# Attention and mixture layer on one core: the projection stage gets x already turned, and normalises it in that layout

## What is computed

```python
def _layernorm(x, axis=-1, eps=1e-05):
    m = jnp.mean(x, axis=axis, keepdims=True)
    v = jnp.var(x, axis=axis, keepdims=True)
    return (x - m) / jnp.sqrt(v + eps)
# x is 2 x 2048 x 512, Wq, Wk, Wv, Wo are 512 x 512, 16 heads of 32
q = split_heads(x @ Wq.T)
k = split_heads(x @ Wk.T)
v = split_heads(x @ Wv.T)
q = _rope(q)
k = _rope(k)
scores = jnp.einsum('bhqd,bhkd->bhqk', q, k) / math.sqrt(dk)   # causal, softmax, @ v, @ Wo.T
x = x + _L0_attn_ref(_layernorm(x, axis=-1), Wq, Wk, Wv, Wo)
x = x + _L0_ffn_ref(_layernorm(x, axis=-1), ...)               # a base product, a router, 8 LoRA experts
```

## Time and profile before

| | us |
|---|---|
| median of 3 runs | 1550.93 |
| lowest and highest | 1549.51, 1551.12 |
| profiled execution | 1550.66 |
| its span | 1548.9 |
| TensorE busy in the span | 1523.7 (98%) |
| VectorE busy | 1132.8 (73%) |
| GpSimd busy | 890.5 (57%) |
| ScalarE busy | 756.4 (49%) |

### The profile page before, as it was taken

One profiled execution on the slowest core, in us unless ns is written; L12 is line 12 of the kernel. 1 busy time (PEld: TensorE's weight loads), 2 busy tenths in 40 slices (PEclk: granted clock), 3 DMA queues, 4 the chain that ended last, 5 costly groups with the idle time before them and its releaser, 6 DMA issues.

```text
span 1548.9 us, 24844 instructions
## 1 busy us (share of the span) xinstructions
PE 1523.7 (98%) x9088; PEld 989.2 (64%) x9088; DVE 1132.8 (73%) x2269; ACT 756.4 (49%) x1540; POOL 890.5 (57%) x597
## 2 busy tenths in 40 slices
PE   7999999999999999999999999999999999999999
PEld 5888887755555555555555555555555547777777
DVE  6765656878877777777777878777777677666655
ACT  3222222135656656666666656665665673232221
POOL 2233332446878788888888797887797721121111
PEclk9999999979999999999999999999999999999999
DMA  5655685782476377468368359358445363223311
GB/s 204 211 190 204 207 266 185 225 187 61 90 167 148 83 160 162 89 140 182 84 137 191 83 127 202 83 116 197 100 99 134 88 147 109 82 82 105 134 61 55
DMA packets 120403, 215.83 MB, mean 139 GB/s; under 512 B 12504, under 2 KB 45784, under 8 KB 113112
## 3 DMA queue, kind: packets, MB, share of 16 engines
q1 hardware_dynamic: 102384, 136.20, 32.6%
q0 software_dynamic: 8064, 58.72, 18.4%
q10 hardware_dynamic: 9840, 19.40, 3.5%
HBM read 96.23 MB, written 58.72 MB: 100 GB/s over the span
## 4 chain that ended last, share of the span: by engine, by line
PE 92%; DVE 4%; DMA 2%; issue 1%; SPq 1%; ACT 1%; POOL 0%; POOLq 0%; DVEq 0%; ACTq 0%
PE a_mx L260 16%; PE a_st L1014 16%; PE a_av L1027 16%; PE p_pair L518 11%; PE f_wo_ps L1370 6%; PE p_v L530 5%; PE f_out_ps L1430 5%; PE a_sum L260 3%; PE a_sum L1049 2%; PE a_sum L1057 2%; DVE a_part L275 2%; PE f_out_ps L1445 1%; PE f_mid_ps L1370 1%; PE f_lg_ps L1400 1%; DMA a_gather<-a_pair 1%; PE a_mx L264 1%
## 5 line engine op out<-in xcount | busy, mean ns | idle before, releaser
L1114 ACT ACTIVATE a_probs<-a_st 128x512 f32<-128x512 f32 (+2 forms) x1244 | 573.6, 547 | 355.9 <-PE a_st L1014 347.2
L275 DVE TENSOR_REDUCE a_part<-a_mx 128x1 f32<-128x512 f32 (+2 forms) x773 | 495.4, 680 | 91.7 <-PE a_mx L260 78.9
L963 POOL TENSOR_TENSOR a_pair<-a_probs 128x1024 f32<-128x1024 f32 (+2 forms) x224 | 401.8, 1835 | 31.7 <-issue 16.4
L963 POOL TENSOR_TENSOR a_gather<-a_probs 128x1024 f32<-128x1024 f32 x76 | 179.9, 2388 | 84.5 <-ACT a_probs L1114 84.5
L392 POOL TENSOR_TENSOR p_rot<-p_mul 128x1024 f32<-128x1024 f32 x32 | 87.5, 2736 | 193.7 <-DVE p_mul L696 193.7
L1363 POOL TENSOR_TENSOR f_x<-f_x,f_bias 128x512 f32<-128x512 f32 x32 | 40.1, 1287 | 204.9 <-DVE f_xn L1580 204.9
L1027 PE MATMUL a_av<-a_probs,a_v 128*32 128x512 f32 (+3 forms) x1280 | 141.0, 540 | 2.2 <-POOL a_probs L944 2.2
L1027 PE MATMUL a_av<-a_probs,shared 128*32 128x512 f32 (+3 forms) x1280 | 142.6, 545 | 0.0
L278 DVE CUSTOM_DVE_ANT_0 a_mx<-a_mx,f_ctx 128x512 f32<-128x512 f32 (+1 forms) x155 | 94.7, 630 | 51.5 <-PE a_mx L260 51.5
L944 POOL TENSOR_SCALAR_AFFINE_SELECT a_probs<-a_probs 128x512 f32<-128x512 f32 x128 | 88.4, 755 | 64.2 <-ACT a_probs L1114 62.3
L1014 PE MATMUL a_st<-a_q_stack,a_k_stack 98*128 98x512 f32 (+3 forms) x287 | 101.8, 372 | 1.1 <-DMA a_q_stack<-a_neg_rows 1.1
(11 more groups left out here) (238 smaller groups left out, 3062.7 us busy)
## 6 DMA issues: line engine op xcount, KB each, us to landing
a_gather<-a_pair POOLq DMA_DIRECT2D x56, 1024.0 KB, 7.2
qk_scratch<-p_rot_hi SPq DMA_DIRECT2D x32, 512.0 KB, 3.1
qk_scratch<-p_rot_lo SPq DMA_DIRECT2D x32, 512.0 KB, 3.9
a_k_stack<-qk_scratch SPq DMA_DIRECT2D x60, 256.0 KB, 8.1
a_q_first<-qk_scratch SPq DMA_DIRECT2D x48, 256.0 KB, 7.0
a_third<-qk_scratch SPq DMA_DIRECT2D x36, 256.0 KB, 5.4
v_scratch<-p_v_st SPq DMA_DIRECT2D x32, 256.0 KB, 7.4
ctx_scratch<-a_ctx_st SPq DMA_DIRECT2D x32, 256.0 KB, 3.5
```

The source lines that it names most:

```text
L275: dve.tensor_reduce(found, scores.rearrange("p (h n) -> p h n", n=width), AX.X, ALU.max).then_inc(self.max_done, 1)
L963: pool.tensor_tensor(place[:, h:h + 2, q0:TT], probs[:, s % RING, h:h + 2, q0:TT], probs[:, (s + 1) % RING, h:h + 2, q0:TT], ALU.add).then ...
L1114: act.activation(probs[:, s % RING, h, q0:TT], score_bank(g, HG * s + h)[:, q0:TT], ACT.Exp, scale=SCORE_SCALE).then_inc(exp_done, 1)
```

## The change

The kernel gets x a second time, turned (features as rows, `x_t`, made like the turned weights before the launch). From tile 1 on: statistics come from `xb`, now one buffer, as before; the reciprocal goes into the variance's place in `mv`, so that mean and reciprocal lie side by side; SP stores `mv` (4 KB) to `row_scratch` in memory, waits for it, and loads it back spread to all 128 partitions as `rows_b` (4 KB in each, `spread_rows`). The turned tile `xt_raw` (1 MB, in the second x buffer's place) is loaded by ScalarE's queue at the end of a tile. GpSimd subtracts the mean from all 2048 elements of a partition in one instruction (`centre`, after rope sum 0), VectorE multiplies by the reciprocal in one (`scale`, after `rot_rest` 0). ScalarE's four `xt_copy` stand together after `rot_copy` 1, VectorE's four `xt_rest` together before `rope_mul` 3, both reading SBUF instead of PSUM. The transposes of tiles 1 to 7 are gone; tile 0 is turned as before.

```diff
-        xb = first.x
+        xb, xt_raw, rows_b = first.x[:, 0], first.x[:, 1], first.cin[:, 2:4, :].rearrange("p a n -> p (a n)")
-        rstd = sb("p_rstd", [P, SUB])
+        rstd = mv[:, :, 1]
+        mean_row, rstd_row = (rows_b.rearrange("q (p s c) -> q s p c", s=SUB, c=2)[:, :, :, c].unsqueeze(1).to_broadcast([P, KT, SUB, P])
+                              for c in range(2))
+        xt_tokens = xt_raw.rearrange("q k (s p) -> q k s p", p=P)
...
+            def centre(T):
+                pool.wait_ge(rows_loaded, 16 * T)
+                pool.wait_ge(xt_loaded, 16 * T)
+                pool.tensor_tensor(xt_tokens, xt_tokens, mean_row, ALU.subtract).then_inc(centred, 1)
             with pool.Fori(0, TILES - 1) as T:
                 for p in range(4):
                     rope_sum(4 * T + p, p % 2)
+                    if p == 0:
+                        centre(T + 1)
...
-            sp.dma_start(xb[:, 1], x_v[1]).then_inc(x_loaded[1], 16)
+            sp.wait_ge(tr_done, KT)
+            sp.dma_start(xb, x_v[1]).then_inc(x_loaded, 16)
+            sp.dma_start(xt_raw, xt_v[1]).then_inc(xt_loaded, 16)
             sp.dma_start(tab[:, 1], rope_v[1]).then_inc(tab_loaded[1], 16)
+            def spread_rows(T):
+                sp.wait_ge(rstd_done, T + 1)
+                if T > 1:
+                    sp.wait_ge(scaled, T - 1)
+                sp.dma_start(row_scr[0].rearrange("(p s) c -> p s c", s=SUB), mv[:, :, :]).then_inc(rows_stored, 16)
+                sp.wait_ge(rows_stored, 16 * T)
+                sp.dma_start(rows_b, row_scr.rearrange("a n c -> a (n c)").to_broadcast([P, 2 * TT])).then_inc(rows_loaded, 16)
             for T in range(TILES - 1):
+                spread_rows(T + 1)
                 for p in range(4):
...
                     v_sub(T, u, p)
-                    if p == 1:
-                        transposes(T + 1, 1 - u, (0, 1))
-                    if p == 2:
-                        transposes(T + 1, 1 - u, (2, 3))
...
+            def load_xt(T):
+                act.wait_ge(xt_lo_done, 4 * T)
+                act.dma_start(xt_raw, xt_v[T]).then_inc(xt_loaded, 16)
             def tile(T, i, u, load):
+                root(T + 1)
                 if load:
-                    load_x(T + 2, u)
-                root(T + 1)
+                    load_x(T + 2)
                 v_copy(T, i, u, 0)
                 rot_copy(T, i, 0)
                 v_copy(T, i, u, 1)
+                rot_copy(T, i, 1)
                 act.wait_ge(v_done, 4 * T + START)
-                for kt in (0, 1):
+                for kt in range(KT):
                     xt_copy(T + 1, 1 - u, kt)
-                rot_copy(T, i, 1)
                 v_copy(T, i, u, 2)
-                for kt in (2, 3):
-                    xt_copy(T + 1, 1 - u, kt)
                 rot_copy(T, i, 2)
                 v_copy(T, i, u, 3)
                 rot_copy(T, i, 3)
                 if load:
+                    load_xt(T + 2)
                     act.wait_ge(mul_done, 4 * T + 4 + AHEAD)
                     load_tab(T + 2, u)
...
+            def scale(T):
+                dve.wait_ge(centred, T)
+                dve.tensor_tensor(xt_tokens, xt_tokens, rstd_row, ALU.mult).then_inc(scaled, 1)
...
                 rope_mul(T, i, u, 0)
                 rope_mul(T, i, u, 1)
                 rot_rest(T, 0)
-                for kt in (0, 1):
-                    xt_rest(T + 1, 1 - u, kt)
+                scale(T + 1)
                 rope_mul(T, i, u, 2)
                 rot_rest(T, 1)
-                for kt in (2, 3):
+                for kt in range(KT):
                     xt_rest(T + 1, 1 - u, kt)
                 rope_mul(T, i, u, 3)
                 rot_rest(T, 2)
```

More of the change, by code:

```diff
@@ L307, in shift_rows, with project @@
                          ).then_inc(self.shift_loaded[t % 2], 16)
-def project(nc, block, x, wq_t, wk_t, wv_t, rope, qk_scr, v_scr, shared, first):
+def project(nc, block, x, x_t, wq_t, wk_t, wv_t, rope, qk_scr, v_scr, shared, first):
     x_v = x.rearrange("(t s p) d -> t p s d", p=P, s=SUB)
+    xt_v = x_t.rearrange("(k p) (t n) -> t p k n", p=P, n=TT)
     rope_v = rope.rearrange("p c (t n) -> t p c n", n=TT)
+    row_scr = nc.dram_tensor("row_scratch", [1, TT, 2], F32, kind="Internal").ap()
     with ExitStack() as ctx:
@@ L342, in turned_x @@
         def turned_x(T, kt):
-            if isinstance(T, int) and T == 0 and kt >= 2:
-                return v_ps[kt % 2]
-            return tr_ps[kt % 2]
+            if isinstance(T, int) and T == 0:
+                return (tr_ps + v_ps)[kt][:, :]
+            return xt_raw[:, kt, :]
         w_loaded = [sem(f"p_w_loaded{n}") for n in range(W_RING)]
@@ L351, in project @@
         zeroed, ident_done = sem("p_zeroed"), sem("p_ident_done")
[L352 removed]
+        x_loaded, xt_loaded, rows_stored, rows_loaded = sem("p_x_loaded"), sem("p_xt_loaded"), sem("p_rows_stored"), sem("p_rows_loaded")
+        centred, scaled = sem("p_centred"), sem("p_scaled")
         first_x = [sem(f"p_first_x{s}") for s in range(SUB)]
@@ L490, in _, with transposes @@
             pe.wait_ge(ident_done, 1)
[L492 to L496, removed]
+            def transposes():
+                pe.wait_ge(xn_done, 1)
+                for kt in range(KT):
                     for s in range(SUB):
-                        mm = pe.transpose(turned_x(T, kt)[:, s * P:(s + 1) * P],
-                                          xb[:, u, s, kt * P:(kt + 1) * P], ident[:, :])
+                        mm = pe.transpose(turned_x(0, kt)[:, s * P:(s + 1) * P], xb[:, s, kt * P:(kt + 1) * P], ident[:, :])
                     mm.then_inc(tr_done, 1)
@@ L574, in last_tile @@
                     v_sub(T, u, s, between)
-            transposes(0, 0, range(KT))
+            transposes()
             for u in range(2):
@@ L597, in xt_copy @@
             def xt_copy(T, u, kt):
-                act.wait_ge(tr_done, 4 * T + kt + 1)
-                act.activation(xt_hi[u][:, kt, :], turned_x(T, kt)[:, :], ACT.Copy).then_inc(xt_hi_done, 1)
+                if isinstance(T, int) and T == 0:
+                    act.wait_ge(tr_done, kt + 1)
+                else:
+                    act.wait_ge(scaled, T)
+                act.activation(xt_hi[u][:, kt, :], turned_x(T, kt), ACT.Copy).then_inc(xt_hi_done, 1)
             def rot_copy(T, i, p):
@@ L1684, in _, with layer @@
                 tile(T, T // 2, T % 2, T < TILES - 1, T < TILES - 2)
-def layer(nc, x, wq_t, wk_t, wv_t, wo_t, rope, base_t, base_b, router_t, router_b, lora_a, lora_b, out):
+def layer(nc, x, x_t, wq_t, wk_t, wv_t, wo_t, rope, base_t, base_b, router_t, router_b, lora_a, lora_b, out):
     qk_scr = nc.dram_tensor("qk_scratch", [4, GROUPS, P, SEQ], F32, kind="Internal").ap()
@@ L1697, in layer @@
         block = ctx.enter_context(nc.Block())
-        project(nc, block, x, wq_t, wk_t, wv_t, rope, qk_scr, v_scr, shared, first)
+        project(nc, block, x, x_t, wq_t, wk_t, wv_t, rope, qk_scr, v_scr, shared, first)
         early.place()
@@ L1725 @@
         "x": np.asarray(L0_attn_x).reshape(TOKENS, DM),
+        "x_t": turned(np.asarray(L0_attn_x).reshape(TOKENS, DM)),
         "wq_t": halves(L0_attn_Wq),
```

22 lines of the change are left out of this document (12 added, 10 removed).

## The result

The changed kernel takes 1643.84 us (median of 6 runs, 1639.44 to 1647.08), the kernel before 1551.03 us (6 runs, 1549.06 to 1552.28). The ratio is 1.060, 95% interval 1.058 to 1.061. The profiled execution took 1640.26 us, its span 1637.8 us against 1548.9 before.

A forecast was written before the change was run, and what follows sets the result against it. TensorE bounds the kernel (35.2 us a tile); the change makes a 44.5 us loop through memory set the tile. Terms 2.2 + 55.8 + 6 + 2.6 + 2.5 = 69.1 on 1550.66 give 1620 us, range 1575 to 1655.

The forecast's parts named there:

- A: The end of a projection tile's last (pair-3) rope product on VectorE, from which the loop's steps are timed in us.
- Store's issue: SP issues the 4 KB mv store at A + 10.0, after the previous tile's last rope store.
- Landing: The 4 KB store reaches memory at A + 21, behind queued stores and 1 MB of x_t; between A + 18 and A + 21.3.
- Broadcast 3.5: Loading the row to 128 partitions (512 KB) takes 3.5 us, so the rows are there at A + 24.5.
- Centre 4.7: GpSimd's mean subtraction over 2048 elements takes 4.7 us; 7.3 if the read every 32 bytes costs extra.
- Centred to A: From centre's end to the next A 15.3 us, GpSimd going first; 13.1 if VectorE wins the first collision, 11 if both.
- 2.2 for tile 1: Tile 1's first trip through memory, rows at 36.8, moves its start from 52.22 to 54.4: +2.2 us.
- 2.5 us for a cold TensorE: TensorE begins the last tile after a gap, so its first products run slowly: +2.5 us once.
- small store that overtakes (1 and 2): Store passes the queue, rows at A + 15.0: 1538.5 us if VectorE wins collisions (8%), about 1551 if it loses (4%).
- milder loop (3): The loop with the queue not pushed and one collision won by VectorE: 38.9 us a tile, 1586 us; 18%.
- dear step (4): The loop with the strided read dear: centre 7.3 us, seven times 2.6 more, 1638 us; 20%.
- clock (5): Gaps of 11 us keep TensorE at half clock for whole tiles: 67 us a tile, about 1740 us; 2%.

The follow-up runs named there:

- Kernel 1: The changed kernel, but only tile 1 sends means and factors through memory and tiles 2 to 7 reuse its row; 1572.03 us.
- kernel 7: Against the version working a tile ahead: row store and broadcast issued apart, statistics earlier, tile 0's first products before scale, attention loads spread; 1545.32 us, ratio 0.997.
- Kernel 5: The changed kernel, but the 1 MB of turned x is loaded for tile 1 only; 1621.22 us.
- kernel 2: The changed kernel, but centre and scale read the row operand as neighbouring elements, not every 32 bytes (wrong values); 1619.74 us.
- kernel 4: The changed kernel, but the 4 KB store and the broadcast load are issued on GpSimd's own queue instead of SyncE's; 1615.71 us.
- kernel 6: The changed kernel a tile ahead: statistics of tile T + 2 taken in tile T, centre before the rope sums, scale after the first rope product; 1563.50 us, ratio 1.007.

## Why the prediction was right, point by point

**The mechanism.** It is the one forecast: a loop through memory that sets the tile, TensorE idle 11 to 12 us in it, GpSimd waiting for the rows. Kernel 1 shows it by taking the trip away. The transposes taken out gave nothing while TensorE waits; kernel 7 shows half of their 12.2 us as won once it doesn't (6.0 at the end of the projection, 3.4 in the span). TensorE idle 11 to 12 us is the tiles in the middle; over all plain tiles its gap is 8.8 to 14.2 us.

**The tile: 44.5 forecast, 47.9 measured.** By steps:
- *Statistics to 1/std, A + 9.3:* A + 9.2.
- *Store's issue, A + 10.0:* A + 12.5. This step failed. I let SyncE be held only until the end of the last rope store's issue as before, and put the added megabyte on the landing alone. With full queues the issues of the rope stores themselves take longer (5.6 us for the two, 3.3 in rows 6). Kernel 5 shows that this is x_t's doing.
- *Landing, A + 21:* A + 21.1. Right by luck, by two errors that cancel: issued 2.5 us late, it needed 8.7 us and not 11. The upper bound was mis-added too: A + 18 and 2.7 us are A + 20.7, not A + 21.3.
- *Broadcast 3.5, rows at A + 24.5:* 4.3, A + 25.4.
- *Centre 4.7, or 7.3 with the step dear:* 6.0. Both values were off, by 1.3 us each way; kernel 2 measures the dense one at 4.6. The Trainium skill ("GPSIMD Engine Reference", section "Performance pitfalls for Q7 kernels") gives reads with a byte step over 8 a rise of one half; here the whole instruction, in which one of two inputs has the step, rises by 29%, from 4.60 to 5.95 us. The direction of the page holds; the forecast should have weighed it higher than one in five.
- *Centred to A, 15.3:* 16.3. GpSimd did go first, as assumed. VectorE's scale took 3.7 us of its own, not 2.2: the same step of 32 bytes, which I had priced on GpSimd and forgotten on VectorE. The other steps were 0.5 us below their sum.

Together 0.9 + 1.3 + 1.0 = 3.2 us of the 3.4 by which the tile is longer.

**The sum: 69.1 forecast, 91 measured to the end of the last pair-3 product.** The first such end moved from 51.9 to 59.9, +8.0, where 2.2 for tile 1 and 2.6 for the product behind the remainders make 4.8; tile 1's rows came at 39.3 and not 36.8, and its centre took 6.1 us. The five plain tiles cost 61.4 us over 35.2 each and not 46.5: 14.9 us, the terms above and a first tile of 50.1, whose rows came at A + 27.6. The tile with the attention's loads cost 21.8 and not 9.3 + 6 = 15.3: its row store was issued at A + 25.9 because single issues on SyncE took up to 7.3 us, a queue so full that it held the engine that feeds it. The 2.5 us for a cold TensorE are not in the sum: the last tile's first item starts 91.1 us late as well, and TensorE waits 1.8 us for it after its slow products, so they had slack there too. In kernel 7, where there is none, the same price is measured (8.19 us for 5.60). Check: 69.1 + 3.2 + 14.9 + 6.5 - 2.5 = 91.2, rounding apart the 91.1 measured. What follows the projection was forecast to give nothing back and gave 2 us.

**The rivals.** A small store that overtakes (1 and 2) is refuted: none of the seven stores landed in less than 4.4 us, the one read here took 8.7 behind the rope stores, and 5.6 on a queue of its own (kernel 4). The milder loop (3) too: the collision that it gave to VectorE went to GpSimd, and the landing was pushed. The dear step (4) came about, at half its price. The clock (5): the granted clock was 0.50 (1.2 GHz) for the first 3.8 to 5.9 us after each gap, then 1.0, never for whole tiles. It slowed products that had 11 us of slack behind them, as the forecast said.

**The range** of 1575 to 1655 held the time because its upper end had the dear centre and a later landing in it. The likeliest time was 24 us low: the loop was 3.4 us short in each tile (broadcast 0.8, centre 1.3, scale 1.5, less 0.5 elsewhere, and the rest in short waits), and tile 1, the first full loop and the tile with the attention's loads had more. The late issue, the largest miss of a single step, did not count, since the landing made up for it; that is luck and not a reading.

## What to carry to other kernels

A change that sends statistics through memory is priced as a loop: follow it once around, from the event that repeats to itself, with every issue in the queue ahead of it, and compare that with the bound engine's time for a tile; an error of 1 us counts as many times as there are tiles. If it is too long, shorten nothing: start it a tile earlier, and put no wait for a landing on a queue that has other stores behind it (the chain of kernel 6 shows the wait; kernel 7 took it out together with three other edits). Price an access with a step on each engine that makes it.

## What the runs showed of the hardware

- A step of 32 bytes in one of two inputs costs both engines: GpSimd 4.60 to 5.95 us for 2048 elements a partition, VectorE 2.1 to 3.7 us beyond the time that it is locked out.
- Issuing a DMA is not of constant cost to its engine. On SyncE a rope store's issue took 0.51 us in quiet, 3.63 in a full window, and with the attention's loads in the queue 7.27, in kernel 1 8.26 and in kernel 4 9.45.
- A 4 KB store took 4.4 to 10.2 us over the tiles of the changed kernel: 8.7 behind 512 KB stores, 9.2 with 1 MB less in the window. On GpSimd's queue it took 5.3 us with the DMA engines half busy and 5.6 with all at work. A 512 KB broadcast took 4.3 us alone, 7.8 beside others.
- After an idle gap of 14.2 us TensorE was granted half its clock for 5.4 us, while working without a pause; after the kernel's other gaps, of 5.5 to 20.1 us, for 3.8 to 5.9 us.
- GpSimd's add of 1024 elements took 5.60 us beside five VectorE operations on SBUF (four of 512 elements, one of 1024), 2.40 alone: over half of its time it was shut out.
